# Scores of the second cross attention in one block, values with 30 columns, and probabilities turned by products with the unit matrix

## What is computed

```python
# second cross attention: x here is the context, cls the normalised rows
kv = (x @ w_kv).reshape(B, Nx, 2, H, D)          # H = 16 heads, D = 8
k, v = ...                                       # (B, H, 64, 8) each
q = transpose((cls @ w_q).reshape(B, N, H, D))
attn = softmax(einsum('bhnd,bhmd->bhnm', q, k) * SCALE)
g = transpose(x @ w_la)
gate = 0.5 * mean(g) + 0.5 * max(g)              # one number per batch and head
attn2 = softmax(gate * attn)
attn = w * attn2 + (1.0 - w) * attn
out = einsum('bhnm,bhmd->bnhd', attn, v) @ w_proj + b_proj
# experts: softmax over 8 logits, top 2 by scores + bias, then
y = sum over e of gate_e * (silu(xt @ w1[e].T) * (xt @ w3[e].T)) @ w2[e].T
z = silu(xt @ sw1.T) * (xt @ sw3.T) @ sw2.T      # out = y + z
```

## Time and profile before

| what | us |
|---|---|
| median of 3 runs | 4233.28 |
| lowest and highest run | 4227.32, 4238.90 |
| the profiled execution, its own time | 4226.67 |
| its span in the trace | 4224.8 |
| TensorE busy | 4047.6 |
| VectorE busy | 3507.6 |
| ScalarE busy | 3012.7 |
| GpSimd busy | 2884.0 |

### The profile page before, as it was taken

One profiled execution on the slowest core, in us unless ns is written; L12 is line 12 of the kernel. 1 busy time (PEld: TensorE's weight loads), 2 busy tenths in 40 slices (PEclk: granted clock), 3 DMA queues, 4 the chain that ended last, 5 costly groups with the idle time before them and its releaser, 6 DMA issues.

```text
span 4224.8 us, 147350 instructions
## 1 busy us (share of the span) xinstructions
PE 4047.6 (96%) x50345; PEld 2794.5 (66%) x50345; DVE 3507.6 (83%) x7187; ACT 3012.7 (71%) x6848; POOL 2884.0 (68%) x3647
## 2 busy tenths in 40 slices
PE   5999998999999999999999999999999999899899
PEld 3777775666666666666666666666666666566565
DVE  4666667999889998899998999899999999577776
ACT  3555556888888888788887888788888888455422
POOL 2333337888878888788887888888888988465400
PEclk9999999999999999999999999999999999887899
DMA  3000001000000001000010001000010000000000
GB/s 90 8 6 7 6 4 48 10 8 9 24 21 9 8 9 33 14 7 10 13 32 9 9 9 29 18 7 10 7 36 10 10 7 8 18 13 11 6 10 10
DMA packets 162234, 64.89 MB, mean 15 GB/s; under 512 B 121557, under 2 KB 156129, under 8 KB 162017
## 3 DMA queue, kind: packets, MB, share of 16 engines
q1 hardware_dynamic: 162016, 62.05, 5.8%
HBM read 26.54 MB, written 2.10 MB: 7 GB/s over the span
## 4 chain that ended last, share of the span: by engine, by line
POOL 42%; PE 27%; issue 22%; DVE 5%; POOLq 2%; SPq 1%; ACT 1%; DVEq 0%; DMA 0%; ACTq 0%
POOL qn L650 11%; POOL qn L639 8%; POOL big L650 7%; POOL e L645 6%; POOL big L639 4%; PE pj L1623 3%; PE pp L1581 2%; PE sc L1883 2%; PE po L1596 2%; PE po L1907 2%; PE sc L1993 2%; PE pj L1615 2%; PE pj L1664 1%; POOL rstd L661 1%; PE po L1602 1%
## 5 line engine op out<-in xcount | busy, mean ns | idle before, releaser
L1690 PE MATMUL pj<-wqkv,xcT 128*128 128x512 f32 x1536 | 800.8, 603 | 17.8 <-issue 9.5
L650 POOL TENSOR_TENSOR qn<-qn,big 128x512 f32<-128x512 f32 x384 | 491.3, 1280 | 294.9 <-DVE big L1209 294.9
L862 ACT ACTIVATE big<-pj 128x512 f32<-128x512 f32 x768 | 474.0, 617 | 69.4 <-PE pj L1690 58.5
L1209 DVE TENSOR_TENSOR big<-pj,ropes 128x512 f32<-128x512 f32 x768 | 522.1, 680 | 0.0
L1215 DVE TENSOR_REDUCE ss<-big 128x8 f32<-128x512 f32 x768 | 515.5, 672 | 0.1
L650 POOL TENSOR_TENSOR big<-big 128x512 f32<-128x512 f32 x384 | 485.9, 1276 | 4.6 <-DVE big L1209 4.6
L1843 PEld LDWEIGHTS pp<-wo,oT 128*128 128x128 f32 x3072 | 357.3, 191 | 161.2 <-ACT oT L885 81.0
L645 POOL TENSOR_TENSOR e<-e,rc 128x512 f32<-128x512 f32 x384 | 401.0, 1044 | 54.4 <-DVE rc L1239 54.4
L639 POOL TENSOR_TENSOR qn<-qn,ny 128x512 f32<-128x512 f32 x384 | 397.3, 1045 | 7.5
L639 POOL TENSOR_TENSOR big<-big,ny 128x512 f32<-128x512 f32 x384 | 396.9, 1045 | 7.6
L1697 PE MATMUL pj<-wqkv,xcT 128*64 128x512 f32 x1536 | 394.8, 614 | 0.8 <-DVE big L1209 0.7
(11 more groups left out here) (320 smaller groups left out, 9976.5 us busy)
## 6 DMA issues: line engine op xcount, KB each, us to landing
wqkv<-in_L_ffn_Wqkv SPq DMA_DIRECT2D x18, 512.0 KB, 3.8
xsd<-Y SPq DMA_DIRECT2D x192, 32.0 KB
xsd<-Y SPq DMA_DIRECT2D x384, 15.8 KB
xsf<-Y SPq DMA_DIRECT2D x96, 64.0 KB
xsf<-Y SPq DMA_DIRECT2D x192, 31.5 KB
xsx<-Y SPq DMA_DIRECT2D x64, 64.0 KB, 1.8
xsx<-CT SPq DMA_DIRECT2D x64, 64.0 KB, 1.9
wo<-in_L_ffn_Wo SPq DMA_DIRECT2D x6, 512.0 KB, 4.4
```

What stands on the lines that cost most here:

```text
L650: nc.gpsimd.tensor_tensor(U[a.par][i], U[a.par][i], t2b[i % 2], ALU.add).then_inc(sem("d_add"), 1)
L862: nc.scalar.activation(sqb[i % 2], pj[i % 2][:, :], ACT.Square).then_inc(sem("d_sq"), 1)
L1209: nc.vector.tensor_tensor(t2v, swapped, sin, ALU.mult).then_inc(sem("d_r"), 1)
L1690: mm(pj[i % 2][:, :], xcT[:, a.par, :], wqkv[:, i * 512:i * 512 + 512], start=True, stop=True).then_inc(sem("d_ch"), 1)
```

## The change

1. **Scores.** `scores(tile, h)` becomes `scores(tile)`: all four products of a tile in a row, at the place in the step where `scores(p[1], 0)` stood. `scores(p[2], 1)` at the head of the step is gone. It waits for both differences of the tile before. The semaphore `l_s` counts once per tile.
2. **Values.** The value blocks and the outputs of `pv` get 30 columns instead of 18; the 12 new columns are zeros and nobody reads them. Gates, logits and row turns move to other columns of their banks.
3. **Turning.** `four` calls the product with the unit matrix in place of the transpose. Its operands are the same: the probabilities are the stationary operand, the unit matrix moves.
4. **The seam.** On VectorE, the normalising of rows 29, 30 and 31 is called earlier, and the 19 routing steps are cut differently around it; `route_rest(0, 2)` moves behind the first two hidden products of the experts. On ScalarE, the exponential of `route_rest` comes before the third Silu instead of before the first; the first group of experts is written out ahead of the loop. On TensorE, `up` of expert 1 stands directly behind `up` of expert 0.

```diff
+        WV = 30
+        l_vall = bq[:, 2048:2048 + 4 * 16 * WV]
+        l_vp = [l_vall[:, 16 * WV * i:16 * WV * i + 16 * WV].rearrange("p (b k c) -> p b k c", b=BT, c=WV) for i in range(4)]
...
-        l_out = [po[i][:, 0:144].rearrange("p (k c) -> p k c", c=18) for i in range(2)]
+        l_out = [po[i][:, 0:8 * WV].rearrange("p (k c) -> p k c", c=WV) for i in range(2)]
...
-            act.wait_ge(sem("r_st"), ROUTE_STEPS + 2)
-            nc.scalar.activation(r_buf[0][:, FIRST:NT, :], r_buf[0][:, FIRST:NT, :], ACT.Exp).then_inc(sem("r_e"), 1)
-
-            with act.Fori(0, NM) as m:
+            def m_group(m, known):
                 for ex in range(NEX):
+                    if known and ex == 2:
+                        act.wait_ge(sem("r_st"), ROUTE_STEPS + 2)
+                        nc.scalar.activation(r_buf[0][:, FIRST:NT, :], r_buf[0][:, FIRST:NT, :], ACT.Exp).then_inc(sem("r_e"), 1)
...
-                        past(dve, "l_s", tile.g * 2 + (h + 1))
+                        past(dve, "l_s", tile.g + 1)
...
-                normalise(p[6])
+                ending = p[3] is None and p[6] is not None
+                if not ending:
+                    normalise(p[6])
...
-                for stage, (first, n) in ROUTED.items():
-                    if p[stage] and isinstance(p[stage].g, int) and p[stage].g == NT - 1:
-                        route(first, n)
+                if p[3] and isinstance(p[3].g, int) and p[3].g == NT - 1:
+                    normalise(p[5])
+                    route(0, 7)
+                if ending and p[4]:
+                    normalise(p[5])
+                    route(7, 10)
+                    normalise(p[4])
+                    route(10, ROUTE_STEPS)
...
-                        route_rest(2 + 2 * ex, 4 + 2 * ex)
+                        route_rest(2 * ex + (ex > 2), 2 * ex + 2 + (ex > 1))
...
-                def scores(tile, h):
-                    if tile:
-                        if h == 0:
-                            past(pe, "l_km", tile.g * 2 + 2)
-                        past(pe, "l_sb1", tile.g * 2 - 1 + h)
+                def scores(tile):
+                    if tile:
+                        past(pe, "l_km", tile.g * 2 + 2)
+                        past(pe, "l_sb1", tile.g * 2)
                         past_waits(pe, "went_on")
-                        r = slice(h * 64, h * 64 + 64)
-                        for bb in range(BT):
-                            q = slice(bb * 64, bb * 64 + 64)
-                            last = mm(sc[q, h * 512:h * 512 + 512], l_kq[tile.par % 2][r, 1, q], l_km[tile.par % 2][r, bb], start=True, stop=True)
+                        for h in range(2):
+                            r = slice(h * 64, h * 64 + 64)
+                            for bb in range(BT):
+                                q = slice(bb * 64, bb * 64 + 64)
+                                last = mm(sc[q, h * 512:h * 512 + 512], l_kq[tile.par % 2][r, 1, q], l_km[tile.par % 2][r, bb], start=True, stop=True)
                         last.then_inc(sem("l_s"), 1)
 
                 def four(bank, src):
                     for j in range(4):
-                        last = nc.tensor.transpose(bank[:, j * P:j * P + P], src[:, j * P:j * P + P], ident)
+                        last = mm(bank[:, j * P:j * P + P], src[:, j * P:j * P + P], ident, start=True, stop=True)
                     return last
...
-                scores(p[2], 1)
                 values2(p[4], p[6])
                 turn1(p[2], 0)
...
-                scores(p[1], 0)
+                scores(p[1])
                 turn2(p[3], 1)
                 tile_turn(p[0])
...
             up(0, True, 0)
+            up(0, True, 1)
```

More of the change, by code:

```diff
@@ L247, in build @@
         l_km = [bq[:, 1024 * i:1024 * i + 1024].rearrange("p (b j t) -> p b j t", b=BT, t=S) for i in range(2)]
-        l_vp = [bq[:, 2048 + 288 * i:2336 + 288 * i].rearrange("p (b k c) -> p b k c", b=BT, c=18) for i in range(4)]
-        l_vall = bq[:, 2048:2048 + 4 * 288]
-        l_ones = l_vall.rearrange("p (x c) -> p x c", c=18)
+        WV = 30
+        l_vall = bq[:, 2048:2048 + 4 * 16 * WV]
+        l_vp = [l_vall[:, 16 * WV * i:16 * WV * i + 16 * WV].rearrange("p (b k c) -> p b k c", b=BT, c=WV) for i in range(4)]
+        l_ones = l_vall.rearrange("p (x c) -> p x c", c=WV)
         l_kq = [kT[:, 2 * i:2 * i + 2, :] for i in range(2)]
         l_pT = [[pT[:, h, :] for h in range(2)], [sqb[h] for h in range(2)]]
-        l_out = [po[i][:, 0:144].rearrange("p (k c) -> p k c", c=18) for i in range(2)]
+        l_out = [po[i][:, 0:8 * WV].rearrange("p (k c) -> p k c", c=WV) for i in range(2)]
         l_gb = [oT[:, i, :] for i in range(2)]
@@ L272, in build @@
         w_turn = [pt_, pp]
-        l_gates, r_logits = po[0][:, 144:144 + L1H], po[0][:, 160:160 + NT * NE].rearrange("p (t x) -> p t x", x=NE)
-        r_rows = po[1][:, 144:144 + 2 * P]
+        l_gates, r_logits = po[0][:, 240:240 + L1H], po[0][:, 256:256 + NT * NE].rearrange("p (t x) -> p t x", x=NE)
+        r_rows = po[1][:, 240:240 + 2 * P]
         r_in = [xsd[:, i, :] for i in range(2)]
@@ L718, in key_rows_masked @@
                             past(pool, "l_kq", tile.g + 1)
-                            past(pool, "l_s", tile.g * 2 - 2)
+                            past(pool, "l_s", tile.g - 1)
                         kk = l_kq[i][:, 0, :].rearrange("p (b t) -> p b t", b=BT)
@@ L974, in keys_queries @@
                         past(act, "l_pj", tile.g + 1)
-                        past(act, "l_s", tile.g * 2 - 2)
+                        past(act, "l_s", tile.g - 1)
                         nc.scalar.copy(l_kq[tile.par % 2].rearrange("p a t -> p (a t)"), pj[0][:, 0:2 * P]).then_inc(sem("l_kq"), 1)
@@ L1066, in _ @@
                     nc.scalar.activation(e[:, ex % 2, :], h_banks[ex % 2][0][:, :], ACT.Silu).then_inc(sem("m_silu"), 1)
+            m_group(0, True)
+            with act.Fori(0, NM - 1) as i:
+                m_group(i + 1, False)
         @block.vector
@@ L1432, in l_step @@
                 aggregate(p[4])
-                for stage, (first, n) in ROUTED.items():
-                    if p[stage] and isinstance(p[stage].g, int) and p[stage].g == NT - 1:
-                        route(first, n)
+                if p[3] and isinstance(p[3].g, int) and p[3].g == NT - 1:
[6 more added lines that the diff above has]
+                    route(10, ROUTE_STEPS)
             tt, reduce, stt = nc.vector.tensor_tensor, nc.vector.tensor_reduce, nc.vector.scalar_tensor_tensor
-            ROUTED = {3: (0, 7), 4: (7, 15), 5: (15, ROUTE_STEPS)}
             def route_step(t, base, n):
@@ L1503, in _ @@
             stream(dve, NT, l_step, 0, 0, 7, 4)
-            route_rest(0, 2)
             acc = oT[:, 0:MT, :]
@@ L2016, in m_group @@
                 for ex in range(NEX):
-                    if ex + 1 < NEX:
+                    if ex + 1 < NEX and (ex or not known):
                         up(m, known, ex + 1)
```

## The result

The changed kernel takes **4207.5 us** (median of four runs, 4204.49 to 4212.11), the kernel before in the same session 4232.3 us (4227.32 to 4238.9): a ratio of 0.9941, 95% interval 0.9924 to 0.9959. That is faster by 0.6%. The profiled execution took 4212.11 us, with a span of 4210.0 us; it is the slowest of its four runs.

What follows compares the result with a forecast made beforehand. TensorE was taken as the bound, lacking full clock; -16.9 us in the 28 steps and -4 at the seam took 4226.7 us to 4206, plus 2 for the median: 4208 us, range 4191 to 4238.

Steps and rivals of the forecast that it cites:

- Turning, +1.76: Four turnings per step: products with the unit matrix need eight records instead of four, adding 0.44 us a call, 1.76 us.
- the waits that shrink, -0.50: Waits around the turnings and L1947 in each step: longer turning and less idle VectorE shorten them by 0.50 us together.
- Scores, -1.01: Score blocks in each step: four products run where two ran, so one block's time, 1.01 us, is saved.
- the new wait, +0.61: Before `values2` in each step: without the removed score block TensorE waits for the copied halves of `pp`, 0.61 us more.
- Rival 3: Score products in the steps still run two at a time, +1.0 us in each of 28, 4236 us; chance 0.06.
- rival 4: The wait for the copy of `pp` is hidden, -0.61 us in each of 28 steps, 4191 us; chance 0.08.
- rival 5: Turnings: each product with the unit matrix is handled as one record, so 28 x -1.76 us or no clock gain; chance 0.03.
- 30 columns, 0: Value blocks in each step: widening from 18 to 30 columns costs 0, with an upper bound of 1.2 us a step.
- The clock, -16.9: The 28 steady steps: full clock throughout, 28 x 10.35 = 289.8 us instead of 306.7, a gain of 16.9 us.
- rival 1: The clock goes on falling as before in the 28 steady steps, a step costs 11.94 us, 4250 us; chance 0.10.
- rival 2: The clock falls half as often in the steps, break-even at 4227 to 4235 us, no change; chance 0.11.
- The seam, -4: Between this attention and the experts: earlier normalising and `up` shorten waits of 3.55 and 2.27 us, gaining 4 us.

## Why the prediction was right, and where not

**The number.** 4208 us were forecast and 4207.5 measured; a step of 10.35 us, and 10.34. That is near in the terms of the work, wrong in what it credits the clock to, and lucky in two places. First, the sum of -21 us went from one profiled execution to the other, and between these the traces show -14.8: 4.9 us are lost ahead of this attention and 0.4 in the fill, and the seam gave 1.2 us less than forecast. The medians lie closer to the forecast because the profiled run before was faster than the four that give its median, and the profiled run of the change the slowest of its four. Second, 9.49 us was read from one step, and once in four steps, a round of the source's loop, TensorE also idles for nothing that the profile shows. The table of waits of the kernel before has it, over the 28 steps:

```profile
PE po L1963 <- issue: 2.9, 8, 0.5
```

At full clock four successive steps of the kernel before take 9.5, 9.5, 9.5 and 10.0 us (read with 30 columns, where the clock is full for longer), four of the change 10.22, 10.21, 10.48 and 10.60. So the usual step grew from 9.49 to 10.21, by 0.72 us where the terms add 0.86; it is the mean, with its longer steps, that met the 10.35.

**Turning, +1.76, and the waits that shrink, -0.50.** Together they make 9.49 + 1.26 = 10.75 us for a step with products alone. The two runs with products and two blocks of scores show 10.66 and 10.68 in the usual step, so the terms are right to 0.1 us. In the changed kernel two of the four calls grew by 0.49 and 0.51 us and the two that had been followed by waits by only 0.27 and 0.22: the longer turning hides what was waited for. And the turning behind L1947, now L1955, starts 0.23 us after it instead of 0.53.

**Scores, -1.01, and the new wait, +0.61.** Together -0.40; undoing the block shows 0.38. By itself the block is as predicted, 1.02 us for eight records. The wait of L1943 comes 1.92 us after the start of the turning, where I had 1.86, and idles for 0.55 us; cutting it gave 0.75 us, a little more than the term. Rival 3, scores two at a time, and rival 4, the wait hidden, both fell; so did rival 5, since each turning has eight records where it had four.

**30 columns, 0.** Right as a cost: 1.12 us for the block, where 1.11 were. The working behind it was circular, though: it took 0.0275 us a record from the difference of the two blocks and then found that eight records of one match eight of the other, which holds whatever the columns cost. But "at this size the columns don't set the pace" made me stop there. Alone they left about a third of the half-clock time of before, 34.1 us of 95.6, and gave 0.7%. I had counted nothing for them on the clock, and that was a step left out.

**The clock, -16.9.** This is the step that failed: "The change turns 16 of these records per step into 32 of real products" was all that I offered for a full clock. The full clock came (0 us of 95.6 at half), and the steps gave -17.3 us. But with transposes it is full as well. The Trainium skill, "TensorE: Matmul & The Clock Gate", Part 4, says that a transpose does not count as busy in the way that a product does; products alone did cut the half-clock time to 13.7 us, which agrees. But the same 16 transposes a step did not keep the clock down where the scores were joined and the columns wide. I took that rule as the reason to believe the sum, and it would have been right to ask which other parts of the change raise the clock for less. The Trainium skill, "Perfetto Trace Analysis", section "Transposes", asks to transpose by transposes and not by products; the runs bear it out, at 1.16 us a step. I had set that rule beside rival 1, a clock that goes on falling; its advice was sound, though rival 1 and rival 2 fell.

**What the products cost.** My own terms for the change without them are 9.49 - 1.01 + 0.61 = 9.09 us, and 9.07 were measured in the usual step, 9.18 in the mean. That sum could have been made before: with a full clock it says that the version without products is 1.26 us a step faster, so that everything hangs on whether it keeps the clock. The prediction never put the two side by side.

**The seam, -4.** Measured -2.8 against the kernel before, and -6.5 against the old order on the changed kernel. The two differ by what I had left out: turnings stand in the seam too, and I had counted products only in the 28 steps. The change with transposes has a seam of 37.9 us against 41.9 with products, before with joint scores and 30 columns 44.2 against 48.4 for the change in its old order: 4 us each time. The last two turnings fall at half clock, where they take 2.07 us as products and 1.06 to 1.12 as transposes. So the term was -6.5 + 4. The waits went as said: 3.55 to 0.77, 2.27 to none.

**The fill, 0,** was +0.4. **The 2 us for the median** rested on the spread between runs being half clock that differs. The runs bear that out for the kernel before: over the 50 on record the slower ones are those with the lower mean clock (4220 to 4229 us at 0.979 to 0.982, 4246 to 4252 at 0.974 to 0.977; correlation -0.84). Part of the spread lies in the stages ahead as well, as the table at the top shows.

**Open.** That joint scores and idle columns raise the clock is shown, why they do is not. Where in the span the half-clock time of the other runs lies is not known either: for them only the mean clock is on record, and by it the kernel before had 152 to 229 us at half clock, an estimate from 2 x (1 - mean clock) x span.

## What to carry to other kernels

When a change is meant to cure a falling clock, price each of its parts alone and at full clock, and try the free ones first: here the dearest part bought nothing that the two cheap ones had not. When a block of work is taken out, look for the copy whose time it covered; if the copy comes in halves, let the reader wait for the halves. Products that use different rows and different columns of the array, issued next to one another, ran four in the time of two.

## What the hardware showed that was not expected

Twelve zero columns more in each of the 32 products of a step cost no time and raised the mean granted clock of the stretch from 0.84 to 0.94. Joining two half blocks of scores into one raised the mean clock from 0.84 to 0.95, although TensorE then does the same products in less time and is idle for longer, 22.8 us of 267.3 against 6.3 of 306.7.
